# Self-attention scores from split F32R operands instead of F32 operands, in a three-stage decoder layer

## The reference

```
q, k, v = x @ wq.T + bq, x @ wk.T + bk, x @ wv.T + bv      # 16 heads of 64
q, k = rope(q, k)
scores = q @ k.T                                            # per head, 1024 x 1024
attn = softmax(where(causal, -inf, scores) / 8)
y = layernorm(x + (attn @ v) @ wo.T + bo)
```

## Time and profile before

| | us |
|---|---|
| three runs: lowest, median, highest | 2109.26, 2111.91, 2113.27 |
| the profiled execution | 2112.43 |
| its span | 2110.7 |

### The profile page before, as it was taken

The page is one execution under the profiler, slowest core; times in us unless marked ns, Lnnn a source line. Parts: engine busy times, 40 slices in busy tenths (PEclk is TensorE's granted clock), DMA queues, the critical chain, the costliest instruction groups (busy, mean ns, idle before and its releaser), DMA issues. The chain is left out here.

```text
span 2110.7 us, 43268 instructions
## 1 busy us (share of the span) xinstructions
PE 1846.8 (88%) x17255; PEld 1127.7 (53%) x17259; DVE 1521.4 (72%) x2147; ACT 1316.2 (62%) x1802; POOL 1496.5 (71%) x1122
## 2 busy tenths in 40 slices
PE   5889999999999999999999999588889898884475
PEld 3545455555555555555455454466677677663333
DVE  6857867868878868878768764257667676777787
ACT  3546656656556656666656655057887877874287
POOL 0767868878868878868778777168768797757256
PEclk8989999999999999999999999679999999997698
DMA  7022122122132032132032020200000000100002
GB/s 226 27 51 66 46 71 66 40 57 66 41 76 66 16 81 66 26 91 66 17 81 66 16 66 27 62 7 8 3 2 8 2 2 2 46 2 2 2 1 80
DMA packets 57511, 92.39 MB, mean 44 GB/s; under 512 B 25312, under 2 KB 35552, under 8 KB 53344
## 3 DMA queue, kind: packets, MB, share of 16 engines
q1 hardware_dynamic: 48096, 89.36, 16.4%
q10 hardware_dynamic: 9216, 0.27, 0.2%
HBM read 51.33 MB, written 4.46 MB: 26 GB/s over the span
## 5 line engine op out<-in xcount | busy, mean ns | idle before, releaser
L947 POOL TENSOR_TENSOR acc<-acc,probs 128x1024 f32<-128x1024 f32 (+3 forms) x320 | 583.0, 1822 | 105.9 <-ACT probs L650 75.4
L650 ACT ACTIVATE probs<-psum 128x1024 f32<-128x1024 f32 (+3 forms) x384 | 290.7, 812 | 162.7 <-PE psum L501 160.7
L594 ACT ACTIVATE chunks<-psum 128x1024 bf16<-128x1024 f32 x288 | 282.0, 1026 | 123.7 <-PE psum L460 78.0
L493 PE MATMUL psum<-operands 64*128 64x512 f32 (+3 forms) x1536 | 309.9, 515 | 17.4 <-ACT chunks L594 16.9
L1523 ACT ACTIVATE onehot<-psum 128x1024 bf16<-128x1024 f32 x320 | 324.5, 1045 | 0.0
L801 DVE TENSOR_REDUCE lows<-chunks 128x2 f32<-128x1024 bf16 (+1 forms) x224 | 266.7, 1217 | 73.4 <-ACT chunks L594 63.5
L517 PE MATMUL psum<-probs,vals 128*64 128x512 f32 (+3 forms) x1536 | 296.1, 503 | 22.5 <-POOL probs L926 12.0
L1353 PE MATMUL psum<-pieces,onehot 128*128 128x64 bf16 x7680 | 281.6, 197 | 14.3 <-ACT vs L1530 13.0
L1353 PEld LDWEIGHTS psum<-pieces,onehot 128*128 128x128 bf16 x7680 | 262.8, 101 | 47.8 <-issue 24.6
L926 POOL TENSOR_SCALAR_AFFINE_SELECT probs<-probs 128x256 f32<-128x256 f32 x256 | 149.2, 600 | 127.5 <-ACT probs L650 127.5
L1994 POOL TENSOR_TENSOR vs<-vs,wgt 128x1280 f32<-128x1280 f32 x64 | 151.9, 2373 | 107.1 <-DVE wgt L1770 102.4
(11 more groups left out here) (243 smaller groups left out, 3397.9 us busy)
## 6 DMA issues: line engine op xcount, KB each, us to landing
operands<-turned SPq DMA_DIRECT2D x124, 256.0 KB, 5.1
rden<-inverse_rows SPq DMA_DIRECT2D x64, 256.0 KB, 3.9
raw<-in_wqk SPq DMA_DIRECT2D x30, 256.0 KB, 4.3
y<-in_x SPq DMA_DIRECT2D x1, 4096.0 KB, 17.9
wo<-in_wo SPq DMA_DIRECT2D x16, 256.0 KB, 2.6
out<-res SPq DMA_DIRECT2D x16, 256.0 KB, 2.1
raw<-in_wv SPq DMA_DIRECT2D x15, 256.0 KB, 4.3
raw<-in_xT SPq DMA_DIRECT2D x12, 256.0 KB, 4.0
```

Of the source, the lines that this page charges most:

```text
L493: nc.tensor.matmul(dst[:, hh, 0:width], ops[n % OBUF][rows, 1, kt * P:(kt + 1) * P].bitcast(F32), ops[n % OBUF][rows, 0, a:a + width].bitc ...
L594: nc.scalar.activation(chunks[k % MBUF][:, :, :], slot("max", n, c)[:, :, :], ACT.Copy, scale=-1.0)\
L650: nc.scalar.activation(probs[u % PBUF][:, :, 0:width], slot("s", n, u)[:, :, 0:width], ACT.Exp, scale=1.0 / D ** 0.5).then_inc(s_exp, 1)
L947: G.tensor_tensor(dst, dst, src, ALU.add).then_inc(s_acc, 1)
```

## The change

Every pair gets a rounded copy of its operands (`high`, two buffers) and the rest in place of the original in `ops`. ScalarE makes the rounded copy in two halves of 2 x 512 elements per partition (`high_operands`), for pair n + 1 in step 0 of pair n, after the exponentials and `copy_out`; it waits there for the operands of pair n + 1 to land. VectorE subtracts it in two halves (`low_operands`), at the end of the steps in LOW_AT: steps 3 and 5 of an even pair, 1 and 2 of an odd one. `scores` becomes three F32R products and waits for both rests before unit 0. The chunks of the maxima are read from `high`.

The two new buffers take 16 KB per partition, so only two batches of rows stay in SBUF during attention (`ends`); the normalised rows of batches 0 and 1 are written to DRAM and loaded again at the start of cross-attention, which now takes the batches in the order 2, 0, 1, 3. The initial load of x is halved, and batches 2 and 3 are loaded later. The rest of the diff renames the rows accordingly, takes the maximum of |y| over three batches with three instructions instead of one of the same total size, and stores the output in the new order.

```diff
+ROWS_ORDER = [2, 0, 1, 3]
+KEPT = 2
+LOW_AT = [(3, 5), (1, 2)]
...
+        high = [sb(f"operands_high{n}", [P, 2, S], F32R) for n in range(2)]
...
+            def load_rows(b):
+                sp.dma_start(batch_tiles(b, 0, TT), dram["x"][b].rearrange("(t p) e -> p t e", p=P)).then_inc(s_y, 16)
+
+            for b in range(2):
+                load_rows(b)
...
+                if i % NG == NG - 1 and 0 < i // NG <= KEPT:
+                    b = i // NG - 1
+                    sp.wait_ge(s_ax1, 2 * (b + 1))
+                    sp.dma_start(kept[b], batch_tiles(b, 0, TT)).then_inc(s_keep, 16)
+                    sp.wait_ge(s_keep, 16 * (b + 1))
+                    load_rows(b + KEPT)
...
             def max_chunk(n, c):
 
-                p = n % OBUF
                 if n == 0 and c == 0:
-                    pe.wait_ge(s_top, 16 * STACK_DMAS)
+                    pe.wait_ge(s_ohi, 1)
                 if c == (2 if n == 0 else 0):
-                    pe.wait_ge(s_ops[p], 16 * STACK_DMAS * (n // OBUF + 1))
+                    pe.wait_ge(s_ohi, 2 * (n + 1))
                 wait_slot(pe, "max", n, c)
                 dst = slot("max", n, c)
                 for qt, hf, col, width in chunk_parts(c):
                     for hh, rows in enumerate(HEADS):
-                        last = nc.tensor.matmul(dst[:, hh, col:col + width], ops[p][rows, 0, qt * P:(qt + 1) * P],
-                                                ops[p][rows, 1, hf * BANK:hf * BANK + width], start=True, stop=True)
+                        last = nc.tensor.matmul(dst[:, hh, col:col + width], high[n % 2][rows, 0, qt * P:(qt + 1) * P],
+                                                high[n % 2][rows, 1, hf * BANK:hf * BANK + width], start=True, stop=True)
                 last.then_inc(s_m, 1)
...
             def scores(n, u):
 
+                if u == 0:
+                    pe.wait_ge(s_olo, 2 * (n + 1))
                 wait_slot(pe, "s", n, u)
                 dst = slot("s", n, u)
                 kt, hf, a, width = span(u)
-                for hh, rows in enumerate(HEADS):
-                    nc.tensor.matmul(dst[:, hh, 0:width], ops[n % OBUF][rows, 1, kt * P:(kt + 1) * P].bitcast(F32),
-                                     ops[n % OBUF][rows, 0, a:a + width].bitcast(F32), start=True, stop=False)
+                hi, lo = high[n % 2], ops[n % OBUF]
+                for term, (k, q) in enumerate(((hi, hi), (hi, lo), (lo, hi))):
+                    for hh, rows in enumerate(HEADS):
+                        nc.tensor.matmul(dst[:, hh, 0:width], k[rows, 1, kt * P:(kt + 1) * P], q[rows, 0, a:a + width],
+                                         start=term == 0, stop=False)
...
+            def high_operands(n, half):
+
+                if n == 0 and half == 0:
+                    act.wait_ge(s_top, 16 * STACK_DMAS)
+                else:
+                    act.wait_ge(s_ops[n % OBUF], 16 * STACK_DMAS * (n // OBUF + 1))
+                if n >= 2:
+                    act.wait_ge(s_s, NU * (n - 1))
+                nc.scalar.activation(high[n % 2][:, :, HALVES[half]], ops[n % OBUF][:, :, HALVES[half]].bitcast(F32),
+                                     ACT.Copy).then_inc(s_ohi, 1)
...
+            high_operands(0, 0)
             for c in range(NCH):
                 copy_chunk(0, c)
+                if c == 0:
+                    high_operands(0, 1)
...
                     if m == 0 and n:
                         copy_out(n - 1, 1)
+                    if m == 0 and n + 1 < PAIRS:
+                        for half in range(2):
+                            high_operands(n + 1, half)
...
+            def low_operands(n, half):
+                x, hi = (t[:, :, HALVES[half]] for t in (ops[n % OBUF], high[n % 2]))
+                dve.wait_ge(s_ohi, 2 * n + half + 1)
+                V.tensor_tensor(x, x.bitcast(F32), hi.bitcast(F32), ALU.subtract).then_inc(s_olo, 1)
...
             negate(0)
+            for half in range(2):
+                low_operands(0, half)
             add_value_bias()
...
+                    if m in LOW_AT[n % 2] and n + 1 < PAIRS:
+                        low_operands(n + 1, LOW_AT[n % 2].index(m))
...
+            for n in range(KEPT):
+                sp.dma_start(y[1 + n], kept[n]).then_inc(s_back[n], 16)
```

More of the change, by code:

```diff
@@ L291, in wait_slot, with batch_tiles @@
                 pe.wait_ge(s_drow, n + 1)
+        def batch_tiles(b, first, last):
+            return ends[:, b % KEPT * TT + first:b % KEPT * TT + last, :]
         def span(u):
@@ L1861, in _ @@
             dve.wait_ge(s_x2, XB - 1)
-            st.then(V.tensor_reduce(hidden.ytop[:, 0:1], y[:, 0:(XB - 1) * TT, :], AX.XY, ALU.max,
-                                    apply_absolute_value=True))
+            for b in range(XB - 1):
+                st.done(V.tensor_reduce(hidden.ytop[:, b:b + 1], y[b], AX.XY, ALU.max, apply_absolute_value=True))
             for t in range(TT):
```

57 lines of the change are left out of this document (36 added, 21 removed).

## The result

| | before | after |
|---|---|---|
| runs on the same chip: median us (lowest, highest) | 2110.59 (2100.65, 2113.27) | 2154.57 (2147.92, 2157.62) |
| ratio, 95% interval | | 1.021 (1.019 to 1.024) |
| span of the profiled execution, us | 2110.7 | 2150.2 |

The account below looks back on a forecast made before the run. TensorE was taken to set most steps, with VectorE hardly behind in even pairs and ScalarE closing step 2. Terms -10 + 18 + 11 + 3.5 = +22.5 us on 2112.43 gave 2135 us, 8-in-10 range 2108 to 2152.

Parts of the forecast that it names:

- What bounds the kernel: TensorE sets most steps, VectorE is hardly behind in even pairs, and ScalarE closes step 2.
- room: VectorE's spare time in an even pair before the next pair's scores, taken as 2.3 us on average.
- The rests on VectorE: Two subtractions per pair at 1.75 us each: +18 us over 14 even pairs (+3 to +44), nothing in odd ones.
- third rival: Subtractions wait until GpSimd's instruction ends, say 2.3 us each: 33 us in place of 18, total 2150; chance 0.15.
- Products: Scores as three F32R products: odd pairs gain about 0.7 us each, -10 us over 14 (-5 to -12).
- Pairs 0 and 1: Pair 1's scores wait for its second subtraction, ScalarE for pair 2's operands: +11 us (+4 to +14).
- Pair 30: No projections and no room; one more subtraction behind its normalisation costs +3.5 us (+2 to +5).
- What would show it: Even-pair score waits of 1 to 2 us ended by L798, VectorE without idle time, periods 40.7 and 39.2, L798 1.5 to 2.0.
- first rival: TensorE is the bound and the rest is covered: its 29 us come in whole, 2083; chance 0.12.

Follow-up runs that it names:

- short_last_additions: Changed kernel with GpSimd's last three additions of the row sums in even pairs cut to 16 columns each; 2139.4 us.
- projection_in_step_4: Changed kernel with the second query and key projection of odd pairs in step 4 rather than 5; 2184.9 us.
- first_rest_left_out: Changed kernel without the first subtraction of even pairs; 2132.6 us.
- no_rests_for_odd_pairs: Changed kernel without both subtractions of every even pair, pair 0 included; 2119.5 us.
- second_half_late_first_in_5: Changed kernel, pair 1's rests formed ahead of pair 0; other odd pairs' second-half subtraction in their own step 0, first half in even step 5; 2129.1 us.
- late_and_ahead: second_half_late_first_in_5 with its one subtraction of even pairs ahead of the normalisation; 2108.7 us.
- late_at_end_of_step_0: late_and_ahead with the second half's subtraction of odd pairs at the end of step 0 rather than its start; 2111.4 us.
- one_product: Changed kernel with the scores' three F32R products replaced by one F32 product of the rounded operands, rests formed but unused; 2158.2 us.

## Why the prediction was wrong in size

*What bounds the kernel.* Right in that VectorE's chain counts in even pairs, TensorE in odd ones. Wrong in what "room" meant. I measured it from VectorE's last instruction to the next score. For the second subtraction this is the right distance. The first stands ahead of GpSimd's mask in time, and the chain rotation, turn, mask, `weigh` had no room before: L517 waited 0.29 us for the mask in pair 18. The text priced that subtraction inside the room and said that `max_row` keeps its own, naming the only waiter on VectorE's own results. With the second one left out, my sum gives 1.5 - 2.3, no cost; 1.28 us were measured, of which 0.8 to 1.0 at full clock; the rest goes with the clock drops.

*The rests on VectorE: the term that failed.* +18 us forecast for even pairs, 32 measured. Each was taken at 1.75 us; measured are 1.50 and 2.86 in even pairs. "Somewhat more" than the mean beside GpSimd was the choice that went wrong: the second does not take a share of GpSimd's load, it stands at a fixed place behind the start of a fixed addition, and pays the rest of it every time. With the measured lengths the sum would have been 1.50 + 2.86 + 0.05 - 2.3 = 2.1 us per even pair, 30 us in all, against 32 found; the closeness is partly luck, as the first goes by another way. By the profile the terms miss by +14 in even pairs, +7 in odd ones, -5 in pairs 0 and 1 and +2 in pair 30, 18 us in all (19.6 in the median): this term is the largest part, and the start's lower cost hides some of it. The third rival (2150, chance 0.15) had the mechanism and 2.3 us for each; measured 2.18 in the mean.

*Products.* Measured on TensorE, from start to start: 0.34 + 0.23 us for the first two products of 512 columns, and the three with the 0.1 us start before 384 columns begin take 0.81 us, the 0.69 predicted and the start. Plain odd pairs gain 0.41, not 0.7, and those with x pieces lose 0.6 each in the mean, 1.8 in pair 21, which this record does not explain: -2.8 in place of -10.

*Pairs 0 and 1.* +5.7 instead of +11. The mechanism is as described: the scores of pair 1 wait for its second subtraction and begin at 103.72 (106.3 said), and in pair 1 ScalarE waits 4.98 us for pair 2's operands (6 said), until 114.2 (116 said). Half of it was made good within pair 1, the lower bound of +4. Rows of PE, and of ACT:

```profile
103.72 0.80 PE L516 MATMUL psum<-operands_high 64*128 64x512 f32 x2 [11.06 <-DVE operands L798]
```

```profile
114.20 2.00 ACT L657 ACTIVATE operands_high<-operands 128x1024 fp32r<-128x1024 f32 x2 [4.98 <-DMA operands<-turned]
```

*Pair 30.* +5.3, just over the bound of 5. Its first subtraction, beside a full GpSimd, took 3.23 us ahead of the row, which `max_row` then waited for; the earlier trace rows had led me to count only the second.

*What would show it.* Idle time before L516 ended by L798, 1 to 2 us, in even pairs only: right, 1.2. VectorE without idle time in even pairs: 40.91 of 42.03, right. Periods of 40.7 and 39.2: 41.0 to 42.5, and 39.3 to 39.9. L798 at 1.5 to 2.0 on average: 1.95, which I had taken for the forecast's sign and which is no sign at all, since it mixes 1.35 to 2.86.

The first rival is refuted in its own terms: TensorE's saved time arrives in odd pairs only. The rule that the third rival quotes from the Trainium skill, "SBUF — State Buffer", section "Who interferes with whom" (a VectorE instruction with two SBUF inputs and a GpSimd instruction that reads SBUF shut each other out for a whole instruction), is borne out by these traces at each place looked at, and in both directions: 1.07 us of work after GpSimd's end, 1.8 us for 32 elements, 178 ns for the same with GpSimd idle, and 1.0 us more for the two masks that meet the first subtraction. The 1.21 us median of the normalisation, which I had set against it, was the instruction that gets in between two additions: in pair 18 before the change it begins at 826.00, the first addition ends at 826.05 and the second begins at 826.19.

## What to carry to other kernels

When an instruction is added to an engine that shares something with another, list not only who waits for its result but what the other engine has to run at that moment and who waits for that. If two engines shut each other out, the price of an instruction depends on its place and hardly on its size: swapping it with a neighbour that nobody awaits gave 13 us here, shrinking it 32-fold the same. A cheaper operation on the busiest engine is worth only what its share of the steps bounds: some 5 of 29 us. And when two placements are compared by whole times, look at the granted clock pair by pair first: here it turned their order round.

## What was not expected of the hardware

TensorE's granted clock was 1.00 (the 2.4 GHz level) in most pairs before and after. The kernel before has a drop in two of the steady pairs, 5 and 13, which have pieces of x; with the change it fell to 0.50 (the 1.2 GHz level) for some 3 us near the end of pairs 6, 14, 24, 26 and 28. In pair 26 TensorE had just stood 1.81 us before L540 (windows of 2 us, columns as above):

```profile
1173.00:1175.00 2.00, 0.51 (x2) 0.23 (x4) 2.00 (x2) 0.58 (x2) 2.00 (x3) 0.95 0.58 115
1175.00:1177.00 2.00, 2.00 (x8) 0.61 (x4) 1.97 (x4) 0.00 (x0) 2.00 (x1) 0.50 0.98 197
```

Pair 10 with the same wait kept its clock, 42.03 us against 42.39. In short_last_additions, where nothing hides it, pair 18 with such a dip took 42.32 and pair 10 without one 40.75: 1.6 us. It explains part of why leaving the second subtraction out gave no more than shrinking it: pairs of that profile at 0.96 on average (6, 10, 18, 22, 24) lost it again.

Over the profiles the drops in even pairs go with the first subtraction's place. With it in step 3 and the three products (projection_in_step_4, which moved other work, apart), `weigh` waits 0.6 to 1.9 us some 35 us into nearly every even pair, and the clock falls in 2 to 7 of the 13; with none in step 3 and the other places as they were (first_rest_left_out, no_rests_for_odd_pairs, second_half_late_first_in_5, late_and_ahead, late_at_end_of_step_0) that wait is at most 0.9 us in these pairs and the clock falls in none or one. In one_product, with the subtraction in step 3 and waits up to 1.27 us, it falls in none. That the wait is the cause is likely and not shown: why one pair has the drop and its twin does not, these runs do not tell.
